# The gate products of a fused attention and expert kernel: high and low half of the gate side by side in one product of sixteen columns, added afterwards by VectorE

## The reference, cut to what matters

```python
x = x + attention(layernorm(x), ctx, ctx, Wq, bq, Wk, bk, Wv, bv, Wo, bo)
x = x + ffn(layernorm(x), gate_w, expert_w)
# ffn
scores = jnp.einsum('bsh,eh->bse', x, gate_w)          # 8 numbers per row
chosen = jnp.argmax(scores, axis=-1)
onehot = jax.nn.one_hot(chosen, gate_w.shape[0], dtype=x.dtype)
expert_out = jnp.einsum('bsh,efh->bsef', x, expert_w)
return x + jnp.einsum('bsef,bse->bsf', expert_out, onehot)
```

## Time and profile before

| | |
|---|---|
| median of 3 runs | 1028.06 us (1027.78 to 1029.04) |
| the profiled execution | 1026.83 us, of which the span of the profile is 1025.1 us |
| mean granted TensorE clock | 0.942 |
| busy: PE, PEld | 923.6 us (90%), 551.0 us (54%) |
| busy: DVE | 778.2 us (76%) |
| busy: ACT, POOL | 554.7 us (54%), 542.3 us (53%) |

### The profile page before, as it was taken

How to read it: one execution, slowest core, us unless ns; L and a number is a source line. 1 busy time by engine, 2 the same in 40 slices (tenths; PEclk the granted TensorE clock), 3 DMA queues, 4 the chain that set the end, 5 groups by cost and what they waited for, 6 DMA issues and landing times. The chain is left out here.

```text
span 1025.1 us, 27401 instructions
## 1 busy us (share of the span) xinstructions
PE 923.6 (90%) x8834; PEld 551.0 (54%) x8835; DVE 778.2 (76%) x1818; ACT 554.7 (54%) x907; POOL 542.3 (53%) x554
## 2 busy tenths in 40 slices
PE   6565889999989999998999999999883999999996
PEld 3232456556565565565655655656653455555553
DVE  7653569889888899897999988988876556556563
ACT  3345767767657677675686776774833112121120
POOL 1150334655564546645555565455443577777774
PEclk9776789999989999998999999999887899999998
DMA  6726322341432323423333243224624355555550
GB/s 203 219 94 183 101 74 64 113 118 49 121 98 72 115 61 115 126 53 99 90 89 115 64 125 115 53 76 121 251 93 166 104 164 170 171 169 160 176 177 26
DMA packets 85687, 121.74 MB, mean 119 GB/s; under 512 B 22849, under 2 KB 49525, under 8 KB 85567
## 3 DMA queue, kind: packets, MB, share of 16 engines
q1 hardware_dynamic: 73359, 84.10, 30.4%
q0 software_dynamic: 11664, 36.05, 9.1%
q10 hardware_dynamic: 544, 0.02, 0.1%
HBM read 57.47 MB, written 39.31 MB: 94 GB/s over the span
## 5 line engine op out<-in xcount | busy, mean ns | idle before, releaser
L839 POOL TENSOR_TENSOR p_lo<-pf,p_hi 77x512 f16<-77x512 f32 x128 | 148.3, 1163 | 233.6 <-ACT p_hi L1183 233.6
L1182 ACT ACTIVATE pf<-scoresT,exp_scale 77x512 f32<-77x512 f32 x256 | 174.6, 682 | 80.9 <-PE scoresT L1017 73.1
L1489 PE MATMUL mo<-e_w,x2T_hi 128*128 x576 | 184.5, 382 | 0.7 <-DVE x2T_lo L1526 0.7
L1183 ACT ACTIVATE p_hi<-scoresT,exp_scale 77x512 f16<-77x512 f32 x256 | 174.8, 683 | 0.0
L1509 ACT ACTIVATE x2T_hi<-mt 128x512 f16<-128x512 f32 x72 | 43.0, 597 | 183.5 <-PE mt L1478 183.5
L1536 DVE SCALAR_TENSOR_TENSOR res<-mo,inv,row 128x512 f32<-128x512 f32 x72 | 54.1, 751 | 91.6 <-PE mo L1489 91.6
L1268 DVE TENSOR_REDUCE negmax<-work 128x4 f32<-128x308 f32 x256 | 112.4, 467 | 6.1 <-PE work L1065 6.0
L1489 PE MATMUL mo<-e_w,x2T_lo 128*128 x288 | 110.0, 382 | 0.0
L839 DVE TENSOR_TENSOR p_lo<-pf,p_hi 77x512 f16<-77x512 f32 x128 | 99.3, 792 | 14.1 <-ACT p_hi L1183 12.0
L1460 POOL DMA_INDIRECT out<-res,row x72 | 71.5, 993 | 65.2 <-DVE xn L1521 57.0
L994 PE MATMUL work<-xnT_hi,wq_hi 128*128 128x512 f16 x256 | 100.3, 392 | 5.6 <-DVE xnT_lo L1246 5.5
(11 more groups left out here) (232 smaller groups left out, 2197.6 us busy)
## 6 DMA issues: line engine op xcount, KB each, us to landing
row<-rows_by_expert SPq DMA_DIRECT2D x72, 257.5 KB
xt<-in_x SPq DMA_DIRECT2D x16, 1024.0 KB, 8.3
q_st<-q_hi SPq DMA_DIRECT2D x256, 64.0 KB, 2.0
pay<-in_L_ffn_expert_w SPq DMA_DIRECT2D x8, 1024.0 KB, 6.3
q_st<-q_lo SPq DMA_DIRECT2D x128, 64.0 KB, 2.0
er<-in_L_ffn_expert_w SPq DMA_DIRECT2D x7, 1024.0 KB, 14.1
k_next<-key_stacks SPq DMA_DIRECT2D x5, 231.0 KB, 9.1
out<-res,row POOLq DMA_INDIRECT x72, 2.7
```

Source lines behind the costliest of these rows:

```text
L839: return tt.tensor_tensor(pp[1][0:LK, g % 2, j, :], pf[:, j, :], pp[0][0:LK, g % 2, j, :], ALU.subtract)
L1182: nc.scalar.activation(pf[:, j, :], sbank[n % SB][0:LK, :], ACT.Exp, scale=exp_scale[0:LK, :])
L1183: nc.scalar.activation(pp[0][0:LK, g % 2, j, :], sbank[n % SB][0:LK, :], ACT.Exp, scale=exp_scale[0:LK, :]).then_inc(sem("exp_done"), 1)
L1489: ins = nc.tensor.matmul(obank2[u % 2][:, :], x2T[ia][:, u % 2, k, :], w, start=k == 0 and n == 0, stop=k == KT - 1 and n == 2)
```

## The change

Both gates are held as one tensor of [128, 4, 2, 8]: for each block of features the 8 columns of the high half, then the 8 of the low half. A product of the data's high half streams all sixteen columns, and gives hi·hi in columns 0 to 7 and hi·lo in columns 8 to 15 of PSUM; the product of the data's low half adds lo·hi into columns 0 to 7. That is 2 products where there were 3, so 32 per stage. VectorE then adds the two groups of eight with a reduction from PSUM (64 inputs, 32 outputs per partition), waits for it, and goes on from SBUF. The hi half stands second in all but the first block of each tile, so the order of products is hi lo, lo hi, lo hi, lo hi.

```diff
-    gt = [sa(f"gate_{s}", [P, KT, E], F16) for s in ("hi", "lo")]
-    wg = [sa(f"wogate_{s}", [P, KT, E], F16) for s in ("hi", "lo")]
+    gt = sa("gate_h", [P, KT, 2, E], F16)
+    wg = sa("wogate_h", [P, KT, 2, E], F16)
...
                     for t in range(TPC):
+                        col = 2 * E * t
                         for k in range(KT):
-                            ins = product(ps[:, t * E:(t + 1) * E], [v[:, k, t * P:(t + 1) * P] for v in a],
-                                          [v[:, k, :] for v in w], k == 0, k == KT - 1)
+                            if k:
+                                nc.tensor.matmul(ps[:, col:col + E], a[1][:, k, t * P:(t + 1) * P], w[:, k, 0, :],
+                                                 start=False, stop=False)
+                            ins = nc.tensor.matmul(ps[:, col:col + 2 * E], a[0][:, k, t * P:(t + 1) * P], w[:, k, :, :],
+                                                   start=k == 0, stop=k == KT - 1)
+                            if k == 0:
+                                nc.tensor.matmul(ps[:, col:col + E], a[1][:, k, t * P:(t + 1) * P], w[:, k, 0, :],
+                                                 start=False, stop=False)
...
-            own = OwnCount(21)
+            own = OwnCount(23)
...
+            def halves(ps):
+                return ps[:, 0:TPC * 2 * E].rearrange("p (t s e) -> p t e s", t=TPC, s=2)
...
-                    do(nc.vector.tensor_tensor(gx[:, n % 2], by_tile(ps), std[:, n % 2, :].unsqueeze(2)
+                    do(nc.vector.tensor_reduce(gx[:, n % 2], halves(ps), X, ALU.add))
+                    do(nc.vector.tensor_tensor(gx[:, n % 2], gx[:, n % 2], std[:, n % 2, :].unsqueeze(2)
                                                .to_broadcast([P, TPC, E]), ALU.mult))
...
                 if kind == "GC":
-                    return nc.vector.scalar_tensor_tensor(out=lg[:], in0=by_tile(ps), scalar=inv_gc[:], in1=gx[:, m.slot % 2],
+                    do(nc.vector.tensor_reduce(lg[:], halves(ps), X, ALU.add))
+                    return nc.vector.scalar_tensor_tensor(out=lg[:], in0=lg[:], scalar=inv_gc[:], in1=gx[:, m.slot % 2],
                                                           op0=ALU.mult, op1=ALU.add)
```

More of the change, by code:

```diff
@@ L574, in _ @@
                     nc.scalar.activation(wgf[:].rearrange("p k e -> p (k e)"), ps[:, 0:KT * E], ACT.Copy)
-                    last = scaled(wg[0][:].rearrange("p k e -> p (k e)"), ps[:, 0:KT * E], S_WG)
+                    last = scaled(wg[:, :, 0, :], ps[:, 0:KT * E].rearrange("p (k e) -> p k e", k=KT), S_WG)
                 last.then_inc(sem("prep_act"), 1)
@@ L678, in gate_split @@
             def gate_split():
-                do(nc.vector.tensor_scalar(gt[0][:], gT[:], scl[:, S_G:S_G + 1], None, ALU.mult))
-                lo(gt[1][:], gT[:], scl[:, S_G:S_G + 1], gt[0][:])
+                do(nc.vector.tensor_scalar(gt[:, :, 0, :], gT[:], scl[:, S_G:S_G + 1], None, ALU.mult))
+                lo(gt[:, :, 1, :], gT[:], scl[:, S_G:S_G + 1], gt[:, :, 0, :])
                 nc.vector.tensor_scalar(bq_s[:], bvec[:, BQ, :], scl[:, S_WQ:S_WQ + 1], None, ALU.mult)
@@ L723, in _ @@
                 elif kind == "wg":
-                    last = lo(wg[1][:].rearrange("p k e -> p (k e)"), ps[:, 0:KT * E], scl[:, S_WG:S_WG + 1],
-                              wg[0][:].rearrange("p k e -> p (k e)"))
+                    last = lo(wg[:, :, 1, :], ps[:, 0:KT * E].rearrange("p (k e) -> p k e", k=KT),
+                              scl[:, S_WG:S_WG + 1], wg[:, :, 0, :])
                 elif kind == "bo":
```

## The result

The changed kernel takes 1046.69 us (median of 4 runs, 1043.78 to 1051.74), the kernel before 1027.92 us beside it (4 runs, 1025.12 to 1029.04). The ratio is 1.0199, 95% interval 1.0155 to 1.0243: 16 to 25 us slower. Forecast were 5.3 us. The profiled execution is the longest of the four, 1051.74 us, so sums over its trace overstate the median's loss by some 5 us.

A forecast was written before the change was run, and what follows sets the result against it. An iteration was taken as a TensorE-VectorE relay. Eleven ordinary iterations at 0.47 us (GC 0.20, GX 0.27) give 5.2, back edges +0.4, last GX +0.1, last GC -0.4: +5.3 us, 1033.4 us; 8-in-10 range 1028.0 to 1035.8.

The forecast's parts named there:

- The relay: Loop iteration: TensorE sets the pace from O0, VectorE from O1 to M03, TensorE from O2 to O3, VectorE to O0.
- Products of 16 columns: Gate stages on TensorE: starts 25 ns apart, so a stage spans 0.8 us where it was 1.2.
- VectorE's wait at O3: Iteration's end: VectorE's 0.35 us wait absorbs its own GC lateness of 0.25, and gets shorter or stays the same.
- The pause that GC's saving turns into: TensorE after GC: the 0.40 us saved becomes a new pause of 0.3 to 0.6 us ahead of M12 and O2.
- The reduction: VectorE, each gate stage: 64 inputs from PSUM take 219 ns, 0.25 us until what follows starts.
- What follows the reduction: VectorE, next instruction: reading SBUF where it read PSUM costs 0.02 us more in GX, nothing more in GC.
- GC's own 0.20: GC stage, each ordinary iteration: O2 has nothing to spare and starts 0.25 - 0.05 = 0.20 us later.
- savings and costs cancel: Rival: O2 need not wait for M03, so TensorE's saving offsets VectorE's cost; near 1029 us, chance 0.14.
- GX's 0.27: GX stage, each ordinary iteration: reduction 0.25 plus SBUF read 0.02 make M33, the halves and O0 0.27 us later.
- Dearer than the line: Rival: the reduction takes over 0.35 us, or new waits lower TensorE's clock; over 1036 us, chance 0.09.
- c = 0.50: Upper bound for the time from reduction to what follows: +11.5 us in all, 1039.6 us.

The follow-up runs named there:

- GC only: The change in stage GC alone, GX left as in the kernel before: 1043.49 us, ratio 1.0148 to the kernel before.
- sum in PSUM: The change, with both reductions writing their sums into the stage's own PSUM bank, read there next: 1033.16 us, ratio 1.0051 to the kernel before.
- sum later: The change without reductions in either stage; existing instructions carry 64 columns, halves added when the expert is chosen: 1027.55 us, ratio 0.9985 to the kernel before.
- no add: The change without reductions, VectorE reading only columns 0 to 7 of each tile: 1027.01 us, ratio 0.9991 to the kernel before.
- experiment 5: The change without reductions, the product with the gate's low half left out of the scores: 1027.01 us, ratio 0.9991 to the kernel before.
- copy in PSUM: Kernel before, 48 products, plus in GC a copy of the scores within their PSUM bank, read there: 1029.63 us, ratio 1.0024.
- copy to SBUF: Kernel before, 48 products, plus in GC a copy of the scores from PSUM to SBUF, read there: 1047.08 us, ratio 1.0184.
- GX only: The change in stage GX alone, GC left as in the kernel before: 1030.75 us, ratio 1.0034 to the kernel before.
- the twelfth kernel: The version adding the halves later, with GX's first result left in its PSUM bank: 1025.72 us, ratio 0.9970 to the kernel before.
- the eleventh: The version adding the halves later, unchanged, measured a second time: 1025.45 us, ratio 0.9970 to the kernel before.
- experiment 1: The change, with both reductions' sums kept in PSUM so the next instruction has one SBUF input: 1033.16 us, ratio 1.0051 to the kernel before.

## Why the prediction was right in sign and wrong in size

To set it beside its own terms I split each of the 11 ordinary iterations at the first products of GX, O0, O2 and the next GX, from the starts in the traces (medians of one trace each, us):

| | GX to O0 | O0 to O2 | O2 to GX |
|---|---|---|---|
| before | 7.70 | 16.96 | 15.23 |
| the change | 8.31 | 18.02 | 15.25 |
| GC only | 7.85 | 18.02 | 15.25 |
| sum in PSUM | 8.32 | 17.09 | 15.25 |
| sum later | 7.88 | 16.89 | 15.23 |
| no add | 7.70 | 16.91 | 15.23 |

**The relay: right, with one wait in another place.** From O2 to GX nothing changes in these kernels, and dropping 16 products in each of the other two parts gives next to nothing (no add: 0.00 and -0.05). Products of 16 columns start 25 ns apart, a stage spans 0.78 us, and VectorE's wait at O3 is 0.35 us as in the earlier trace rows. The pause that GC's saving turns into was foreseen ahead of M12 and O2; it stands ahead of M10, for Q1's low half (experiment 5), and the pauses at M12 and O2 of the change come from the long instruction and the reduction.

**The reduction: right.** 206 and 212 ns against 219.

**What follows the reduction: the step that failed.** The prediction said "What follows the reduction now reads SBUF where it read PSUM", put it at 0.02 us more in GX and at nothing in GC, and went on: "then the sum into `lg`, then M03's reduction, each 0.20 later than now". It took the price from a like instruction that reads SBUF at 192 ns; in all 16 stages GpSimd runs nothing beside that one. In GC the step costs 0.94 us more (1.19 instead of 0.25), and O0 to O2 grows by 1.06 us, not 0.20. With the sum in PSUM, where that step costs what the prediction gave it, the kernel measured +5.2 us (3.1 to 7.5) against a forecast of +5.3. That it fits so well is in part luck, since two smaller misses, told below, cancel. A sign of the wait was shown: in the earlier trace rows the second instruction of GX takes 0.35 us, and it has two SBUF inputs and GpSimd's copy of the keys beside it; the one in the earlier trace rows, with one, takes 0.25. The prediction used the row for its starts and passed over its length. In the kernel after it is GX's first instruction that meets the copy:

```profile
431.86 0.32 DVE L1287 TENSOR_TENSOR gx<-gx,std 128x32 f32<-128x32 f32 x1
432.22 0.25 DVE L1289 SCALAR_TENSOR_TENSOR gx<-gx,inv,gate_c 128x32 f32<-128x32 f32 x1
```

**GC's own 0.20: too much by some 0.07.** The prediction let O2 start "with nothing to spare" because it came 0.14 us after M03's bank was free. O2's weight load and first product with the sum in PSUM, where M03's reduction ends at 445.28:

```profile
445.33 0.10 PEld L994 LDWEIGHTS work<-wo_hi,cT_hi 128*128 128x128 f16 x1 [0.29 <-DVE negmax L1281]
```

```profile
445.33 0.39 PE L994 MATMUL work<-wo_hi,cT_hi 128*128 128x512 f16 x1
```

So where O2 truly waits for VectorE it starts 0.06 us behind it, in 13 of the 14 stages. In the trace before it started 0.13 us behind M12, as closely as M12 behind M11, and had 0.09 us to spare: a piece of the rival "savings and costs cancel". O0 to O2 grows by 0.13 us with the sum in PSUM, over some 13 iterations 0.9 us less than forecast, and by 0.19 with the copy in PSUM.

**GX's 0.27: right in three of four, short in one.** With the sum in PSUM GX to O0 grows by 0.24 to 0.27 us in most iterations. In one of four, three times in all, it grows by 0.61, from 7.70 to the 8.31 or 8.32 that is the median: there VectorE stands still for 0.33 us behind GX's last instruction, put down to issue. It is so in the change and with the sum in PSUM. The other kernels of the table do not have it: in the same iteration GC only has 0.15 us more than before and sum later 0.18, no add nothing. No run shows what it is. In the change itself one more iteration of four grows by 0.36, where the row above meets GpSimd's copy.

**The rivals.** "Dearer than the line" named the range that came true, over 1036 us, but by a reduction over 0.35 us or by the clock. The reduction was not it; the clock did fall in O2, but only behind the long instruction and for the smaller part of the loss. By the prediction's own terms c = 0.50 gives +11.8 and not +11.5; nothing hangs on it. In the traces with the long instruction (the change, GC only, copy to SBUF) two to three O2 stages each run at half clock, 1.5 to 1.7 us apiece; in the traces of before, GX only, sum in PSUM, sum later, no add and copy in PSUM none does in the loop's full iterations. The sum then: forecast 5.3 us, 13 long stages at about 0.85 us more (1.06 less the 0.20 forecast), 11 us, three pauses of 0.33, 1 us, make 17 us, and the clock's three stages in the profiled execution 5 us more, 22. Measured were 16 to 25; how often the clock fell in the other executions no trace shows.

**Left open.** Why the later sum comes out ahead of before. In its two profiles the time from the second GX stage to the end is 892.9 us each, before 896.3; 2.5 us of that lie behind the last GX stage. Part of these 2.5 us is the clock: O0 of the last two iterations takes 2.69 us from first to last product before and 2.37 in the two profiles. But the twelfth kernel, as fast, has 896.0 us in all and 3.1 to 3.2 us for these two O0. Nor does the mean clock of the runs tell them apart: 0.944 for the eleventh, the twelfth and the kernel before beside them. And the first profile of the later sum is of the fastest of its twelve executions, 1022.88 us. No run separates these. Nor did a run take GpSimd's low halves away from GC; that two SBUF inputs alone are harmless rests on the last two GC stages of the change, at 0.25 us, and on GX's second instruction, at 0.25 us in the 12 stages of the trace before in which GpSimd was idle.

## What to carry to other kernels

Before an operand of a VectorE instruction moves from PSUM to SBUF, count the SBUF inputs of the instruction and look at what GpSimd runs in the same microsecond: a second SBUF input made 0.25 us into up to 1.19, as much as GpSimd's instruction was long. If a sum must be made between two instructions, leave the sum in PSUM, or better widen the instructions that are there and add where nobody waits. And where two engines hand work to each other, products saved on the one that is waiting anyway are worth next to nothing until the other's part gets shorter: here 12.9 us of them measured 3 us at most.

## What the runs showed of the hardware

- VectorE instructions with two inputs in SBUF waited for GpSimd's running one: 1.10 to 1.20 us instead of 0.25 in 13 of 16 stages, ending 0.05 us after GpSimd did. With one input in PSUM (experiment 1): 0.25 us, though it started 0.01 us behind the same GpSimd instruction. GpSimd's own 1.15 us did not grow.
- It was there in every kernel: VectorE's own low halves, with both inputs in SBUF, take 0.67 to 0.69 us alone and up to 2.0 us in the trace before beside GpSimd's additions; 1.70 us in this place of the kernel after:

```profile
402.01 1.70 DVE L839 TENSOR_TENSOR p_lo<-pf,p_hi 77x512 f16<-77x512 f32 x1
```

```profile
400.64 2.50 POOL L931 TENSOR_TENSOR xt<-xt,bo_rep 128x512 f32<-128x512 f32 x2
```

- On VectorE 32 columns more in a running instruction cost 0.02 to 0.03 us, an instruction of its own with its wait 0.25.
- A TensorE that had waited 0.7 us for M12 and again for O2 sometimes ran the next O stage at half clock, 4.07 us instead of 2.37, and sometimes not, in otherwise alike iterations. It may be what spreads the four executions from 1043.8 to 1051.7 us, since the two longest have the lowest mean clock (0.935 and 0.940, the others 0.943 and 0.945), but only the longest has a trace.
